# Four attention score columns carried in the source table of a graph network's first attention pass

## The reference

```python
x_l = (x @ W_l + b_l).reshape(n, H, C)
x_r = (x @ W_r + b_r).reshape(n, H, C)
e = jax.nn.leaky_relu(x_l[src] + x_r[dst], NEG_SLOPE)          # 0.2
logits = jnp.einsum('ehc,hc->eh', e, att)
m = jax.ops.segment_max(logits, dst, num_segments=n)
p = jnp.exp(logits - m[dst])
alpha = p / (segment_sum(p, dst)[dst] + 1e-16)
out = jax.ops.segment_sum(x_l[src] * alpha[:, :, None], dst, num_segments=n)
```

## Time and profile before

| | |
|---|---|
| median of 3 runs | 7910.9 us (7909.47 to 7912.47) |
| span of the profiled execution | 7912.9 us |
| POOL busy | 5523.4 us (70% of the span) |
| PE busy | 4838.3 us (61%) |
| DVE busy | 4476.8 us (57%) |
| ACT busy | 2097.8 us (27%) |

### The profile page before, as it was taken

How to read it: one execution, slowest core, us unless ns; L and a number is a source line. 1 busy time by engine, 2 the same in 40 slices (tenths; PEclk the granted TensorE clock), 3 DMA queues, 4 the chain that set the end, 5 groups by cost and what they waited for, 6 DMA issues and landing times. The chain is left out here.

```text
span 7912.9 us, 112109 instructions
## 1 busy us (share of the span) xinstructions
PE 4838.3 (61%) x32954; PEld 3963.3 (50%) x32954; DVE 4476.8 (57%) x15028; ACT 2097.8 (27%) x4735; POOL 5523.4 (70%) x5311
## 2 busy tenths in 40 slices
PE   4799887666666547777656566664555556444442
PEld 3466665566556446666635455553444444333332
DVE  9999998677777653333346666665444443111113
ACT  9454443122222241111121111112232223111110
POOL 0477777577777557777757788774777774777775
PEclk9999999788888755555577766766565558555555
DMA  0122221566666446666557766762555553333333
GB/s 15 32 56 55 53 53 35 157 162 161 158 162 160 107 87 134 134 136 134 127 149 203 205 198 200 207 197 66 156 156 156 156 156 87 99 104 104 105 104 80
DMA packets 1304014, 990.39 MB, mean 125 GB/s; under 512 B 287713, under 2 KB 1192995, under 8 KB 1303411
## 3 DMA queue, kind: packets, MB, share of 16 engines
q0 software_dynamic: 183088, 352.33, 18.0%
q1 hardware_dynamic: 700995, 378.63, 17.1%
q10 hardware_dynamic: 419328, 252.26, 11.6%
HBM read 613.75 MB, written 368.79 MB: 124 GB/s over the span
## 5 line engine op out<-in xcount | busy, mean ns | idle before, releaser
L983 POOL DMA_INDIRECT l_rows<-tab,by_src x1664 | 1813.0, 1090 | 611.0 <-issue 506.6
L983 POOL DMA_INDIRECT l_rows<-tab,by_dst x832 | 974.0, 1171 | 324.8 <-issue 237.2
L983 POOL DMA_INDIRECT l3a_rows<-tab,by_dst x832 | 804.4, 967 | 297.1 <-issue 253.3
L983 POOL DMA_INDIRECT l3b_rows<-tab,by_dst x832 | 793.5, 954 | 294.4 <-issue 253.2
L802 POOL DMA_INDIRECT sorted_dst<-pay,place_i x783 | 792.3, 1012 | 275.3 <-issue 237.8
L1129 PE MATMUL l_ps_z<-l_win,l_sel_t 128*128 128x128 f32 x3328 | 758.0, 355 | 204.6 <-DMA l_rows<-tab,by_dst 178.3
L1430 PE MATMUL l3b_ps_o<-l3b_rows,l3b_sel 128*128 128x128 f32 x1664 | 425.7, 437 | 631.3 <-DMA l3b_rows<-tab,by_dst 631.3
L1129 PEld LDWEIGHTS l_ps_z<-l_win,l_sel_t 128*128 128x128 f32 x3328 | 609.8, 251 | 227.9 <-issue 171.6
L1430 PEld LDWEIGHTS l3b_ps_o<-l3b_rows,l3b_sel 128*128 128x128 f32 x1664 | 370.5, 328 | 686.9 <-issue 686.9
L1430 PE MATMUL l3a_ps_o<-l3a_rows,l3a_sel 128*128 128x128 f32 x1664 | 402.2, 417 | 484.5 <-DMA l3a_rows<-tab,by_dst 484.5
L1457 DVE TENSOR_SCALAR l3b_sel<-iota,by_dst 128x128 f32<-128x128 f16 x832 | 186.1, 303 | 859.3 <-PE l3b_ps_o L1430 855.7
(11 more groups left out here) (423 smaller groups left out, 12349.8 us busy)
## 6 DMA issues: line engine op xcount, KB each, us to landing
parts<-l_sums ACTq DMA_DIRECT2D x416, 264.0 KB
l_win<-win SPq DMA_DIRECT2D x1664, 64.0 KB
parts<-l3a_sums SPq DMA_DIRECT2D x208, 512.0 KB, 3.0
l_row<-slot_rows ACTq DMA_DIRECT2D x624, 128.0 KB, 3.2
parts<-l_sums ACTq DMA_DIRECT2D x208, 272.0 KB, 4.0
parts<-l3b_sums SPq DMA_DIRECT2D x208, 256.0 KB, 2.4
low_bc<-lo_rows SPq DMA_DIRECT2D x194, 256.0 KB
l_rows<-tab,by_src POOLq DMA_INDIRECT x1664
```

The lines of the kernel that those rows point to most:

```text
L983: pool.indirect_dma_start(rows[:, q, g, :], None, table, bass.IndirectOffsetOnAxis(ap=index[:, k * G + g:k * G + g + 1], axis=0))\
```

## The change

In the first layer the score att . leaky(z) is written as att . (0.2 z) + (0.8 att) . max(z, 0). Of the first term the part of x_r[dst] is the same for every edge of a destination and falls out of the softmax, so only the part of x_l[src] stays: four numbers for each source node, one for each head.

- `load_step` makes them as four more columns of the product: `c.w0` gets four columns (0.2 att times W_l, summed over each head's channels) in its middle, `load_bias` too. `tab0` grows from 128 to 132 columns, so that a gathered row has 528 bytes in place of 512.
- In the pass, ACT's Relu (L1161) goes; in its place ACT copies the 4 x 4 gathered numbers of the group before into a 33rd column of `l_prod` (L1182 of the changed kernel). DVE's two operations L1208 and L1217 become one, max(z, 0) times `l_att` straight from PSUM (L1231), and the sum for the scores runs over 33 elements (L1262). The tile `l_z` goes; the head of the pass gets a tile `l_same` and a scaled copy of `att`.
- The l2 pass keeps its operations.

```diff
         def _(act):
             act.wait_ge(bias_ps, 1)
-            act.activation(bias_bc[:], po[1], ACT.Copy).then_inc(bias_done, 1)
+            act.activation(bias_bc[:, 0:D], po[1][:, 0:D], ACT.Copy).then_inc(bias_done, 1)
+            act.activation(bias_bc[:, D + HEADS:], po[1][:, D:2 * D], ACT.Copy).then_inc(bias_done, 1)
...
+            dve.scalar_tensor_tensor(lean[:, 0], c.w0[:, 0:D], LEAK, c.att[:], ALU.mult, ALU.mult).then_inc(leaned, 1)
             dve.memset(c.x[:, full], 0.0).then_inc(x_zero, 1)
+            dve.wait_ge(leaned, 1)
+            dve.tensor_reduce(c.w0[:, D:D + HEADS], lean[:, 0].rearrange("p (h c) -> p h c", h=HEADS), AX.X, ALU.add)\
+               .then_inc(lean_done, 1)
...
+            dve.scalar_tensor_tensor(lean[:, 1], bias_bc[:, 0:D], LEAK, c.att[:], ALU.mult, ALU.mult)\
+               .then_inc(leaned, 1)
+            dve.wait_ge(leaned, 2)
+            dve.tensor_reduce(bias_bc[:, D:D + HEADS], lean[:, 1].rearrange("p (h c) -> p h c", h=HEADS), AX.X,
+                              ALU.add).then_inc(lean_done, 1)
...
-    rw = 2 * D if dot else D
-    v0 = rw - D
+    rw = 2 * D if dot else D + heads
+    v0 = D if dot else 0
+    pw = width if dot else width + 1
...
-        z = kit.sb(f"{name}_z", [P, 2, G * D])
-        prod = kit.sb(f"{name}_prod", [P, 2, G * D])
+        prod = kit.sb(f"{name}_prod", [P, 2, G, heads, pw])
+        att = kit.sb(f"{name}_att", [P, D]) if not dot else None
...
-        z_free = prod_done if dot else leaky_done
...
-                    wait_count(pe, z_free, k - 1)
+                    wait_count(pe, prod_done, k - 1)
...
-                            mm = pe.matmul(ps_z[k % 2][:, g], c.ident[:], rows[:, q, g], start=False, stop=True)
+                            mm = pe.matmul(ps_z[k % 2][:, g], c.ident[:], rows[:, q, g, 0:D], start=False, stop=True)
...
-                if k < GROUPS and not dot:
-                    act.wait_ge(z_done, k + 1)
-                    wait_count(act, prod_done, k - 1)
-                    act.activation(z[:, k % 2], ps_z[k % 2].rearrange("p g d -> p (g d)"), ACT.Relu, scale=1.0 - LEAK)\
-                       .then_inc(relu_done, 1)
+                if 0 <= k - 1 < GROUPS and not dot:
+                    j = k - 1
+                    act.wait_ge(landed[j % RING], landed_before[j % RING] + 16 * G * (j // RING + 1))
+                    if j < 2:
+                        act.wait_ge(bounds, 5)
+                    wait_count(act, score_done, j - 1)
+                    act.activation(prod[:, j % 2, :, :, width], rows[:, j % RING, :, D:], ACT.Copy)\
+                       .then_inc(flat_done, 1)
...
+            if not dot:
+                dve.tensor_single_scalar(att[:], c.att[:], 1.0 - LEAK, ALU.mult).then_inc(att_done, 1)
...
-                        dve.wait_ge(relu_done, j + 1)
-                        of = z[:, j % 2].rearrange("p (g d) -> p g d", g=G)
-                        dve.scalar_tensor_tensor(of, ps_z[j % 2], LEAK, of, ALU.mult, ALU.add).then_inc(leaky_done, 1)
+                        dve.wait_ge(z_done, j + 1)
+                        dve.scalar_tensor_tensor(prod[:, j % 2, :, :, 0:width],
+                                                 ps_z[j % 2].rearrange("p g (h d) -> p g h d", h=heads), 0.0,
+                                                 replicate(att[:].rearrange("p (h d) -> p h d", h=heads), 1, G),
+                                                 ALU.max, ALU.mult).then_inc(prod_done, 1)
...
-                if 0 <= k - 1 < GROUPS and not dot:
-                    j = k - 1
-                    dve.wait_ge(leaky_done, j + 1)
-                    dve.tensor_tensor(prod[:, j % 2].rearrange("p (g d) -> p g d", g=G),
-                                      z[:, j % 2].rearrange("p (g d) -> p g d", g=G),
-                                      replicate(c.att[:], 1, G), ALU.mult).then_inc(prod_done, 1)
...
                     dve.wait_ge(prod_done, j + 1)
+                    if not dot:
+                        dve.wait_ge(flat_done, j + 1)
...
-    tab0, tab1, tab2 = dram("tab0", (NP, D)), dram("tab1", (NP, D + 4)), dram("tab2", (NP, 2 * D))
+    tab0, tab1, tab2 = dram("tab0", (NP, D + HEADS)), dram("tab1", (NP, D + 4)), dram("tab2", (NP, 2 * D))
```

More of the change, by code:

```diff
@@ L826, in load_step @@
         xt = kit.sb("load_xt", [P, 2, G, P])
-        tab = kit.sb("load_tab", [P, 2, CB, 2 * D])
-        bias_bc = kit.sb("load_bias", [P, 2 * D])
+        tw = 2 * D + HEADS
+        tab = kit.sb("load_tab", [P, 2, CB, tw])
+        bias_bc = kit.sb("load_bias", [P, tw])
+        lean = kit.sb("load_lean", [P, 2, D])
         px = [kit.ps(f"load_px{i}", [P, G, P]) for i in range(2)]
-        po = [kit.ps(f"load_po{i}", [P, 2 * D]) for i in range(2)]
+        po = [kit.ps(f"load_po{i}", [P, tw]) for i in range(2)]
         ps_end = kit.ps("load_ps_end", [NT, 2, P])
@@ L860, in _ @@
                 sp.wait_ge(tab_done, (j + 1) * CB)
-                for table, c0 in ((tab0, 0), (c.win0, D)):
+                for table, c0, c1 in ((tab0, 0, D + HEADS), (c.win0, D + HEADS, tw)):
                     sp.dma_start(table[j * CB * P:(j + 1) * CB * P, :].rearrange("(i p) d -> p i d", p=P),
-                                 tab[:, j % 2, :, c0:c0 + D]).then_inc(stored[j % 2], 16)
+                                 tab[:, j % 2, :, c0:c1]).then_inc(stored[j % 2], 16)
             for b in range(2):
@@ L869, in _ @@
         def _(pe):
-            pe.matmul(po[1], c.one_rows[:], c.bias_rows[:, 0:2 * D], start=True, stop=True).then_inc(bias_ps, 1)
+            pe.matmul(po[1][:, 0:2 * D], c.one_rows[:], c.bias_rows[:, 0:2 * D], start=True, stop=True)\
+              .then_inc(bias_ps, 1)
             pe.wait_ge(ends, 3)
@@ L1036 @@
 OB = 4
+HEADS = 4
 def attention_pass(nc, c, name, key, heads, dot, table, window_table, runs, slot_rows):
@@ L1069, in attention_pass @@
         sums = kit.sb(f"{name}_sums", [P, OB, G, w])
-        last = prod[0:8].rearrange("p j d -> p (j d)")[:, 0:T]
-        same = z[0:8].rearrange("p j d -> p (j d)")[:, 0:T]
+        last = prod[0:8].rearrange("p j g h d -> p (j g h d)")[:, 0:T]
+        same = kit.sb(f"{name}_same", [8, T])
         ps_z = [kit.ps(f"{name}_ps_z{i}", [P, G, D]) for i in range(2)]
@@ L1075, in attention_pass @@
         ps_o = [kit.ps(f"{name}_ps_o{i}", [P, 2, 512]) for i in range(2)]
-        (sel_t_done, z_done, relu_done, leaky_done, prod_done, score_done, score_ps, prefix_done, top_done, diff_done, exp_done,
+        (sel_t_done, z_done, flat_done, att_done, prod_done, score_done, score_ps, prefix_done, top_done, diff_done, exp_done,
          weight_ps, weight_done, val_done, sums_ps, sums_done, masks, bounds) = (
             kit.sem(f"{name}_{n}") for n in
-            ("sel_t_done", "z_done", "relu_done", "leaky_done", "prod_done", "score_done", "score_ps", "prefix_done", "top_done",
+            ("sel_t_done", "z_done", "flat_done", "att_done", "prod_done", "score_done", "score_ps", "prefix_done", "top_done",
              "diff_done", "exp_done", "weight_ps", "weight_done", "val_done", "sums_ps", "sums_done", "masks",
@@ L1233, in _ @@
                     dve.tensor_tensor(val[:, j % 2, :, 0:D].rearrange("p g (h d) -> p g h d", h=heads),
-                                      rows[:, j % RING, :, v0:].rearrange("p g (h d) -> p g h d", h=heads),
+                                      rows[:, j % RING, :, v0:v0 + D].rearrange("p g (h d) -> p g h d", h=heads),
                                       replicate(val[:, j % 2, :, D:w], 3, width), ALU.mult).then_inc(val_done, 1)
@@ L1238, in _ @@
                     dve.wait_ge(prod_done, j + 1)
+                    if not dot:
+                        dve.wait_ge(flat_done, j + 1)
                     wait_count(dve, score_ps, j - 1)
-                    dve.tensor_reduce(score[:, j % 2], prod[:, j % 2].rearrange("p (g d) -> p g d", g=hg),
+                    dve.tensor_reduce(score[:, j % 2], prod[:, j % 2].rearrange("p g h d -> p (g h) d"),
                                       AX.X, ALU.add).then_inc(score_done, 1)
```

15 lines of the change are left out of this document (10 added, 5 removed).

## The result

| | before | after |
|---|---|---|
| median | 7910.2 us (7899.8 to 7912.5, 4 runs) | 8011.3 us (7998.6 to 8013.1, 4 runs) |
| profiled span | 7912.9 us | 8010.5 us |

The ratio is 1.0126, with a 95% interval of 1.0114 to 1.0138: the changed kernel is 1.3% slower. I had forecast 0.8% faster, 7849 us.

A forecast was written before the change was run, and what follows sets the result against it. POOL's gathers, lengthened by DVE operations with two SBUF inputs, were taken to bound l0. Holds -62, load step +1, longer rows 0 and pass ends -1 us gave 7851 on the span, 7849 us median; range 7812 to 7960.

The forecast's parts named there:

- What bounds the pass: In l0, POOL waits for nobody; the pass lasts as long as its 832 gathers, losing 0.88 us per group.
- The mechanism of the hold: A gather waits for DVE operations with two SBUF inputs, the last of a gapless run, then needs 0.83 us more.
- What the prediction worked out from the rule: In l0, L1229 with one SBUF input never holds, so the gap is open in all groups: -89 to -70 us.
- `l_val` no longer waits: In l0, ACT's weights are there by 2.8 us, so l_val follows L1229 without waiting, as in the l2 pass.
- I take: The choice, for the new l0, of the l2 iteration where a gather got in between l_sel and l_val.
- the gap term: In l0, with the gap ahead of l_val open, hold falls from 0.88 to 0.58 us per group: -62 us.
- The earlier trace: Kernel before, l2: the gather at 4328.26 got in, ending 0.98 us behind l_sel, 0.15 us later than usual.
- Rival 1: In l0 the gap ahead of l_val is shut: one run of 1.83 us, 1.11 us per group, +48 us; chance 0.25.
- rival 1 and worse: In l0, the case that the new product holds gathers despite its PSUM input, 0.65 us more of run.
- factor 0.77: Kernel before, l0: measured hold of 0.88 us per group against 1.15 reckoned with arbitrary phase.
- by phase: Hold reckoned for requests every 1.25 us at arbitrary phase; 1.21 us per group for a run of 1.83 us.
- longer rows and load step: Rows of 528 bytes cost 0, at the worst 14 us; evictions and small operations of the load step +1 us.

The follow-up runs named there:

- e5: Changed kernel, with l_val in the l0 pass reading the weights from PSUM instead of ACT's copy in SBUF; 7834.8 us, ratio 0.9911.
- e6: e5 with l_val reading the weights from PSUM in the l2 pass too; 7701.1 us, ratio 0.9733; measured again 7699.4 us, 0.9727.
- e10: e7 with l_sel made by four operations with one SBUF tensor and a pointer; 7601.2 us, 0.9599; in two earlier measurements 1.0279 and 1.0303.
- e2: Changed kernel, with the score sum of the l0 pass moved from behind l_val to ahead of it; 7945.3 us, ratio 1.0032.
- e3: Kernel before, with only ACT's order in the l0 pass changed, the weights' copy ahead of Relu; 8089.8 us, ratio 1.0218.
- e1: Changed kernel, with ACT again waiting for z of the newest group ahead of the weights' copy in l0; 7853.9 us, ratio 0.9913.
- e8: Changed kernel, with the small copy edge_top moved between l_diff and l_val in l0; 7898.3 us, ratio 0.9984.
- e7: e6 with l_prefix written to PSUM too, so that l_top reads one SBUF tensor; 7706.1 us, ratio 0.9736.
- e4: Kernel before, with the changed kernel's load step and 132 columns, four of them gathered and not used; 7917.3 us, ratio 0.9996.
- e9: e6 with l_sel made by four operations with one SBUF tensor and a pointer; 9416.6 us (1.0276) and 9598.2 us (1.0330).
- e11: Kernel before, with weights and l_prefix in PSUM and l_sel made by four operations; 7680.2 us, 0.9698; in two earlier measurements 1.0462 and 1.0421.

## Why the prediction was wrong

- **What bounds the pass** was right: the loss and every gain above stand in the gathers' duration, and the l0 pass grew by as much as its gathers did (111 and 110.6 us).
- **The mechanism of the hold** was right for the operations with two tensors in SBUF, and e5, e6 and e10 show it, not only the timelines: with the second input out of SBUF `l_val` and `l_top` hold little or nothing. The rule of the Trainium skill (page "SBUF — State Buffer", section "Who interferes with whom") agrees for `l_sel` and `l_val`. It doesn't settle `l_sel_t`, which reads one tensor in SBUF and holds gathers for 51 us in e2: the rule leaves out the 2-port modes, and no run here shows in which mode `l_sel_t` ran. What the prediction worked out from the rule, that `l_diff` with one SBUF input leaves the gap open, gave -89 to -70 us and doesn't agree with the measurement: +98 us on the span.
- **`l_val` no longer waits** was right: DVE waits for ACT ahead of it for 1.4 us in the whole program, where it was 303.8. e3 shows that this alone costs 2.2% in the kernel before, and e1 that taking it back turns the change into a gain of 0.9%.
- **The step that failed is "I take"**: that the gap of 0.13 us between `l_sel` and `l_val` is open when the product ahead has stood ready. The product did stand ready each time, and yet only 1 of 163 gathers got in. So the gap term, -0.30 us per group and -62 us, came out as +0.56 us per group (1.44 against 0.88) in the stretch and +110.6 us over the pass. The earlier trace rows was no stray row. In the l2 pass of the kernel before, 37 of 179 gathers that start near `l_sel` (as near as counted under e8) get in; these are 37 of the 42 ahead of which the product stood ready, and 0 of 137 where it had waited. What the prediction overlooked is that in those 42 DVE hadn't waited at `l_prefix` or `l_sel_t` of that iteration either, while in the new l0 pass it had in all 163. Whether that wait is the cause no run tested, and what decides stays open. The one gather of l0 that got in (start 2417.56) fits another reading, that the gap stays shut when `l_val` already stands ready: ACT's weights came 0.17 us ahead of `l_val`, later than in any of the others. e8 shows the bound: 0.20 us of gap, with one operation more in it, lets most in.
- **Rival 1 was the case, but its term, 1.11 us per group and +48 us, was mis-sized**: measured 1.44 us in the stretch, and 110.6 us in all. (7957 us, given for it, should be 7959 by the prediction's own terms.) Two things were missing. The hold reaches back into the second half of the product (14 of 39), which the prediction named as a way to be "rival 1 and worse". e7 and e10 differ in `l_sel` alone and show whose hold it is: gathers asking in `l_top` with one SBUF input are held 26 of 26, by 0.79 us, where `l_sel` holds behind it, and 20 of 36, by 0.11 us on average, where it doesn't; in the product it is 22 of 43 and 0 of 65. And the phase isn't arbitrary. Of the 249 gathers of the new l0 pass that start within 1 us ahead of `l_sel` or 0.7 us behind its start, 60 start 0.17 or 0.18 us ahead of it. My reading, which no run tested alone, is that a held gather restarts the sequence of 1.25 us at the end of the run, so that the next iterations meet it at the same place. That works for a kernel (before: factor 0.77) or against it (1.44 against 1.21 by phase: a factor of 1.19).
- **The smaller terms**: longer rows and load step at 0 to 1 us were right as far as can be measured (e4: 0.9996; 49 evictions of 427 ns). DVE fell by 97 us, not 135, ACT by 84 of 85, and neither moved the time, as said. The 13 us that l2 gained were not foreseen. With the same code that pass took between 1241 and 1268 us in the kernel before, the changed one, e1 to e5 and e8, so 13 us is within what it varies by.
- **The chances**: rival 1 had 0.25 with the earlier trace rows speaking for it in the pass that has this very order. Two rows that differ, neither explained, didn't carry 0.60 for either.

## What to carry to other kernels

Where GpSimd issues indirect gathers back to back and bounds a stage, look at VectorE for operations with two SBUF tensors, and at how closely they follow each other; moving one operand to PSUM (e6: -2.7%) or to a pointer (with that, e10: -4.0%) costs VectorE 0 to 0.3 us a group and gives most of the gathers' time back. A wait of an engine off the path can be what keeps such operations apart: before removing one, ask what closes up behind it (e3: +2.2%). Measure such an edit where it will run: e10 was 4.0% faster than the kernel before at one time and 3% slower at two others. A gain measured on one order can have the other sign on another: the same change gave +1.3% here and -1.0% (7601.2 against 7680.2 us) once the other holds were gone.

## What the runs showed of the hardware

- An undisturbed indirect gather of 128 rows took 0.95 us and 0.30 us of issue, with rows of 512 bytes and of 528 (1.170 and 1.175 us on average in the same pass with holds). One held by an operation on VectorE ended 0.83 us behind the end of that operation.
- A gather's hold begins ahead of the operation that holds: with `l_sel` next behind `l_top` (one SBUF input, e7), gathers asking in `l_top` (26 of 26) and in the second half of the product (22 of 43 in all of it) are held to the end of `l_sel`.
- A gap of 0.13 us between two such operations let in 1 of 163 waiting gathers in l0 of the changed kernel, and 37 of 179 in l2 of the kernel before, all of these where VectorE hadn't waited in that iteration. One of 0.20 us with an operation more let in 134 of 148 (e8), and then the gather ends 0.98 us behind the first operation instead of 0.83.
- Operations with one SBUF tensor and a pointer hold too: `l_sel_t` (0.47 us, where operations of its shape with two tensors take 0.65) holds 92 gathers for 51 us in the l0 pass of e2, 52 for 22 us in that of e8 and 86 for 19 us in the l2 pass of e10. The gather again ends 0.83 us behind its end.
- The same kernel can take very different times: the kernel before took 9177 and 9300 us in the first two measurements of e9 to e11 and 7917 us in the third. The first and the third ran on the same chip (number 8), so the chip alone doesn't explain it; the cause stays open. In the slow two the order of e10 and before is reversed, while e10 and e11 keep theirs (0.982 and 0.985 against 0.990).
